# Second front of a hybrid attention and expert block: statistics, slot tables, row numbers and shared products in another order

## The reference, cut to what matters

```
x = x + attn_a(layernorm(x))      # a linear attention with decays, 16 heads of 8
x = x + ffn(layernorm(x))         # first feed-forward step
x = x + attn_b(layernorm(x))      # block attention on 5 levels, 16 heads of 64
x = x + ffn(layernorm(x))         # second feed-forward step, the same weights

def ffn(h):                                       # h: 2048 x 128
    shared = (silu(h @ shared_gate_w) * (h @ shared_up_w)) @ shared_down_w
    logits = h @ gate_w                           # 32 experts
    e, top = argmax(logits), max(logits)
    hs = h * sigmoid(top)
    routed = (silu(hs @ gate[e]) * (hs @ up[e])) @ down[e]
    return shared + routed
```

## Time and profile before

| what | value |
|---|---|
| runs | 557.72, 559.16, 559.17 us |
| profiled execution, its own time | 557.5 us |
| its span, first to last instruction | 555.6 us |
| TensorE busy | 495.6 us, 89% |
| VectorE busy | 425.7 us, 77% |
| ScalarE busy | 291.0 us, 52% |
| GpSimd busy | 251.4 us, 45% |
| mean granted TensorE clock | 0.979 |
| first products of the second loop | at 497.1 us |

### The profile page before, as it was taken

How to read it: one execution, slowest core, us unless ns; L and a number is a source line. 1 busy time by engine, 2 the same in 40 slices (tenths; PEclk the granted TensorE clock), 3 DMA queues, 4 the chain that set the end, 5 groups by cost and what they waited for, 6 DMA issues and landing times.

```text
span 555.6 us, 16703 instructions
## 1 busy us (share of the span) xinstructions
PE 495.6 (89%) x6472; PEld 304.0 (55%) x6472; DVE 425.7 (77%) x979; ACT 291.0 (52%) x624; POOL 251.4 (45%) x294
## 2 busy tenths in 40 slices
PE   6989888897989997999999999999999868989991
PEld 3323232355444443777767777777767655544540
DVE  3386968988747766868899888899878988847762
ACT  3544344254448864666545555446644433448870
POOL 3556777555514545253344443333233435633542
PEclk9999999999999999999999999999999988999996
DMA  6799920000269862100000000000000000169964
GB/s 183 313 425 283 99 21 0 2 0 20 76 190 268 271 216 72 30 4 21 21 21 22 22 22 22 22 21 21 22 21 8 7 2 11 42 187 275 276 217 139
DMA packets 45326, 54.11 MB, mean 97 GB/s; under 512 B 10880, under 2 KB 36416, under 8 KB 44224
## 3 DMA queue, kind: packets, MB, share of 16 engines
q1 hardware_dynamic: 42688, 47.78, 29.6%
q0 software_dynamic: 2560, 5.26, 2.7%
HBM read 43.55 MB, written 9.48 MB: 95 GB/s over the span
## 4 chain that ended last, share of the span: by engine, by line
PE 59%; DVE 24%; issue 6%; DMA 4%; POOL 3%; ACT 2%; DVEq 0%; SPq 0%; POOLq 0%; ACTq 0%
PE psum L1249 9%; PE psum L1730 7%; PE psum L1748 7%; PE psum L1823 5%; PE psum L1802 4%; PE psum L1268 4%; PE psum L1256 3%; DVE arena L761 3%; POOL sorted_x L1467 2%; PE psum L1771 2%; DVE arena L755 2%; PE psum L277 2%; PE psum L278 2%; DVE arena L2032 2%; DVE arena L2027 2%
## 5 line engine op out<-in xcount | busy, mean ns | idle before, releaser
L2202 POOL TENSOR_TENSOR arena<-arena 128x512 f32<-128x512 f32 x32 | 40.9, 1297 | 110.2 <-issue 103.0
L1495 POOL DMA_INDIRECT y_tok<-arena,to x48 | 46.6, 971 | 64.8 <-ACT arena L1318 63.4
L1918 ACT ACTIVATE arena<-psum 128x512 f32<-128x512 f32 x64 | 37.9, 597 | 45.2 <-PE psum L1730 42.0
L1730 PE MATMUL psum<-arena 128*128 128x512 f32 x128 | 59.2, 605 | 0.8 <-ACT arena L1901 0.7
L1249 PE MATMUL psum<-experts,arena 128*32 x96 | 50.2, 604 | 1.1 <-ACT arena L1308 1.1
L1249 PE MATMUL psum<-arena 128*32 128x512 f32 x288 | 50.9, 605 | 0.0
L661 POOL TENSOR_TENSOR arena<-arena 128x512 f32<-128x512 f32 x32 | 37.2, 1181 | 26.2 <-DVE arena L761 17.5
L1748 PE MATMUL psum<-arena 128*128 128x128 f32 x384 | 47.5, 278 | 1.4 <-ACT arena L1923 1.4
L1748 PEld LDWEIGHTS psum<-arena 128*128 128x128 f32 x384 | 45.2, 191 | 2.4 <-ACT arena L1923 2.4
L2139 POOL TENSOR_TENSOR arena<-arena 128x256 f32<-128x256 f32 (+4 forms) x75 | 33.9, 452 | 24.5 <-ACT arena L1937 17.9
L1730 PEld LDWEIGHTS psum<-arena 128*128 128x128 f32 x128 | 22.9, 189 | 35.6 <-issue 34.0
(11 more groups left out here) (240 smaller groups left out, 1204.1 us busy)
## 6 DMA issues: line engine op xcount, KB each, us to landing
arena<-in_experts SPq DMA_DIRECT2D x48, 384.0 KB, 4.4
experts<-in_experts SPq DMA_DIRECT2D x8, 1536.0 KB, 17.4
arena<-sorted_x SPq DMA_DIRECT2D x48, 64.5 KB, 3.8
sorted_x<-zeros SPq DMA_DIRECT2D x2, 1536.0 KB, 13.4
arena<-in_w_qkv SPq DMA_DIRECT2D x16, 192.0 KB, 3.4
arena<-y_tok SPq DMA_DIRECT2D x8, 256.0 KB, 3.1
x_tok<-in_x SPq DMA_DIRECT2D x4, 256.0 KB, 4.9
arena<-in_w_out SPq DMA_DIRECT2D x16, 64.0 KB, 1.9
```

The source lines that it names most:

```text
L1495: pool.indirect_dma_start(out=y_tok, out_offset=bass.IndirectOffsetOnAxis(ap=f_to[:, s:s + 1], axis=0), in_=f_gy[(s + 4) % 8], in_offset=N ...
L1730: pe.matmul(ring("in", n, j)[:, :], b_w[n % 2][:, which * P:which * P + P], x, start=True, stop=True)\
L1918: act.activation((b_q, b_k)[which][:, part * CHUNK:part * CHUNK + CHUNK], src, ACT.Copy, scale=(D_B ** -0.5, 1.0)[which]).then_inc(h["drai ...
L2202: pool.tensor_tensor(b_yn[:, part], b_y[:, part], b_rec[:, part], ALU.mult).then_inc(h["normed"], 1)
```

## The change

All of it is in the second front (k = 1) and in the last step of the second attention; the first front keeps its order. On TensorE one half of shared chunk 0 goes ahead of `project_out(15)`, the logits of chunk 2 go between the two turns, one half of shared chunk 1 goes ahead of the count, `shared_out(0)` goes behind the count, the two `keep_clock` products go, and the turn of line 1216 goes behind `shared_out(1)`. On GpSimd the second half of the last multiply of line 2202 goes; VectorE does it as `normalise_late`, with a signal of its own. On VectorE `first_slots` goes behind the statistics of chunk 3, one product of shared chunk 0 goes ahead of `gather_out`, `first_rows` goes behind the norm of chunk 3, and the search for the slots' experts, now a function `slot_experts`, goes behind `add_shared(0)` and the products of shared chunk 1. On ScalarE the second silu of shared chunk 0 goes ahead of the norm of chunk 2.

```
@@ TensorE, f_pe
                 front_turn(pe, k, 2)
+                front_logits(pe, k, 2)
                 front_turn(pe, k, 3)
-                front_logits(pe, k, 2)
                 front_logits(pe, k, 3)
+                shared_half(pe, k, 1, 0, 1)
+            count_tokens(pe, k, 1)
+            if k == 0:
+                shared_half(pe, k, 1, 0, 1)
+            else:
                 shared_out(pe, k, 0)
-            count_tokens(pe, k, 1)
-            shared_half(pe, k, 1, 0, 1)
             shared_half(pe, k, 1, 1, 2)
-            keep_clock(2)
+            if k == 0:
+                keep_clock(2)
             shared_half(pe, k, 2, 0)
+            if k == 1:
+                shared_out(pe, k, 1)
             done(pe, "slot_col", 1)
             pe.matmul(bank[7][0:1, 0:P], f_slot_col, ident, start=True, stop=True).then_inc(t["slot_row"], 1)
-            shared_out(pe, k, 1)
+            if k == 0:
+                shared_out(pe, k, 1)
@@ ScalarE, f_act
                 gate_shared(act, k, 0, 0)
+                gate_shared(act, k, 0, 1)
                 front_norm(act, k, 2)
-                gate_shared(act, k, 0, 1)
@@ VectorE, second_places: what followed row_numbers(dve, chain, a, 1) is now
+        def slot_experts(dve, chain, k):
+            before, a = half_of(k, 0), half_of(k, 1)
@@ VectorE, f_dve
                 row_ids(dve, k)
-                first_rows(dve, chain, k)
             c = STEPS - 1
...
             ins.then_inc(t["xn_last"], 1)
             if k == 1:
+                first_rows(dve, chain, k)
+                route(dve, chain, k, 2, 2)
+                product_shared(dve, k, 0, 1)
+                second_places(dve, chain, k)
+                add_shared(dve, k, 0)
                 for n in range(2):
-                    product_shared(dve, k, 0, n)
-                route(dve, chain, k, 2, 2)
+                    product_shared(dve, k, 1, n)
+                slot_experts(dve, chain, k)
@@ TensorE, project_out(n)
-                        pe.wait_ge(h["normed"], 2 * n + i // 4 + 1)
+                        if n == LAST and i:
+                            pe.wait_ge(h["normed_late"], 1)
+                        else:
+                            pe.wait_ge(h["normed"], 2 * n + i // 4 + 1)
@@ TensorE, last step of b_pe
+                    pe.wait_ge(h["y_out"], UNITS)
+                    shared_half(pe, 1, 0, 0)
                     project_out(n - 1)
-                    pe.wait_ge(h["y_out"], UNITS)
-                    for half in range(2):
-                        shared_half(pe, 1, 0, half)
+                    shared_half(pe, 1, 0, 1)
@@ VectorE, b_dve
+            def normalise_late():
+                part = slice(CHUNK, SEQ)
+                dve.wait_ge(h["y_out"], UNITS)
+                dve.wait_ge(h["o"], 2 * LAST)
+                dve.tensor_tensor(b_yn[:, part], b_y[:, part], b_rec[:, part], ALU.mult).then_inc(h["normed_late"], 1)
...
                 if n == UNITS:
-                    first_slots(dve, chain, 1)
+                    normalise_late()
+                    product_shared(dve, 1, 0, 0)
...
+            first_slots(dve, chain, 1)
             dve.wait_ge(h["acc"], 2 * LAST)
@@ GpSimd, b_pool_engine
-                for j in range(2):
+                for j in range(2 if n < LAST else 1):
```

More of the change, by code:

```diff
@@ L51 @@
 FOUND = 4
-SLOT_BOUND = "second_places keeps the expert of a slot between 0 and EXPERTS - 1"
+SLOT_BOUND = "slot_experts keeps the expert of a slot between 0 and EXPERTS - 1"
 ROW = C + 1
@@ L1374, in f_dve @@
                 route(dve, chain, k, 3, 1)
[L1375 to L1378, removed]
+                add_shared(dve, k, 0)
+                second_places(dve, chain, k)
+                slot_experts(dve, chain, k)
+                for n in range(2):
+                    product_shared(dve, k, 1, n)
             done(dve, "slot_row", 1)
@@ L1593, in hybrid_block @@
             "shift xn xt x pooled packed packed_odd ready coarse proj drained scored subbed turned expd weighed merged summed y_out z_out divided normed o biased "
-            "acc logits_in").split()}
+            "acc logits_in normed_late").split()}
         w_in, wo_in, bias_in = [sem(f"b_w_in{r}") for r in range(2)], [sem(f"b_wo_in{r}") for r in range(2)], sem("b_bias_in")
```

## The result

The changed kernel is slower. Its median is 561.79 us of 21 runs (559.59 to 564.21); the kernel before, run beside it, has 558.56 us of 21 (555.83 to 561.41). The ratio is 1.0058, with a 95% interval from 1.0043 to 1.0074: 3.2 us more. Of the versions further down, one run each of 3 (1660.38 us) and 11 (590.14) and one of the kernel before (967.94) were slow and are not in the ratios. The prediction had 559.2 us and no change as the likeliest case. The loss by late weight loads was in its sum, but at a size that cancelled against a gain.

A forecast was written before the change was run, and what follows sets the result against it. The landing of the last indirect write (493.82) lets the second loop start. GpSimd's gain of 0.6 us and SyncE's loss of 0.85 cancel, shift 0.0, so the median of 559.16 gives 559.2 us; range 556.8 to 561.0.

The forecast's parts named there:

- The attention's end: End of the second attention: `normalise_late` 1.31 us and a shared product 0.65 on VectorE; `gather_out` at 460.1, 1.25 earlier.
- `first_slots` in its new place: On VectorE behind chunk 3's statistics, without GpSimd's large multiply beside it: 1.9 us instead of 3.40, ending at 466.3.
- rival (c): Slower: `first_slots` keeps its 3.4 us and the last write lands 1.2 late, 560.4 us; chance 0.13.
- `placed` 1: VectorE's signal ahead of GpSimd's first eight writes: 1.7 us later, near 469.7, with the first write at 470.55.
- The turns and logits: Chunks 2 and 3 on TensorE in the second front: `route` starts at 470.9, gaining 1.05 us (0.45 to 1.6).
- the forecast's best case of 1.6: Turns and logits of the second front all at the full clock: `route` at 470.35, gain 1.6 us.
- GpSimd's queue as the bound: Sixteen writes without a pause: ninth at 481.3, 0.6 us earlier, last issued at 490.2; a pause before the ninth refutes it.
- Shared work last: Second front, search behind shared products: slots' row ready at 484.3, SyncE's weight loads start at 485.75, 0.85 us later.
- The landing: Last indirect write, issued 4.4 us after the loads' start, lands 8.1 after it, at 493.85 against 493.82 before.
- (a): Loads don't hold the writes: the last write lands 3.05 us after its issue, 558.6 to 558.0 us; chance 0.25.
- (b): Queue bounds fall altogether: ninth write follows `placed` 2 at its best, 1.6 earlier, with shorter fetch; 557.5 us; chance 0.15.
- Rival (d): Clock falls in TensorE's shared chain behind 1.35 us idle: 0.2 to 0.9 late, 559.4 to 560.1 us; chance 0.12.

The follow-up runs named there:

- 3: Changed kernel plus three products of 512 columns on TensorE in its idle time ahead of chunk 2's turn: ratio 1.0015 to the kernel before, median 559.17 us.
- 11: Version 5 (early search and products ahead of chunk 2's turn) timed again: ratio 0.9968 to the kernel before, median 557.57 us.
- 1: Changed kernel with the slots' experts searched early again and their row turned ahead of `shared_out(1)`: ratio 1.0003 to the kernel before, median 558.55 us.
- 2: Kernel before with only the late search of the slots' experts and their row turned behind `shared_out(1)`: ratio 1.0040, median 560.75 us.
- experiment 4: Changed kernel plus three products of 512 columns on TensorE between the last `shared_out` and the loop: ratio 1.0024 to the kernel before, median 560.02 us.
- 5: Changed kernel with the early search and three products on TensorE ahead of chunk 2's turn: ratio 0.9978 to the kernel before, median 558.14 us.
- 9: Changed kernel, search left late, with three products ahead of chunk 2's turn and three ahead of the loop: ratio 0.9995 to the kernel before, median 558.36 us.
- version 10: Changed kernel with early search, three products ahead of chunk 2's turn and the two `keep_clock` products put back: ratio 0.9985 to the kernel before, median 558.27 us.

## Why the prediction was wrong, point by point

- **The attention's end: right.** The half of chunk 0 took 1.88 in the gap, `normalise_late` 1.34 (1.31 forecast), and `gather_out` came at 459.54, which is 1.23 earlier when the offset of 0.58 at the entry is taken out (1.25 forecast).
- **`first_slots` in its new place: right.** From 463.86 to 465.74, 1.88 us (1.9 forecast). The scan took 0.68 and line 1092 0.19, so they are short away from GpSimd's multiply, and rival (c) falls. This agrees with the rule of the Trainium skill on the port pair of VectorE and GpSimd (SBUF — State Buffer, on the two separate sides of SBUF). So does `normalise_late`, which has two SBUF inputs, stands beside GpSimd's multiply and took 1.34, but no run shows it alone.
- **`placed` 1: right,** 469.1, and 469.7 with the offset, as forecast.
- **The turns and logits: the mechanism right, the term mis-sized.** The forecast had a stretch at the lower level from 467 to 470 and put `route` at 470.9. The clock fell as soon as forecast but stayed down until 477, through the logits of both chunks and the turn between. They took 1.70, 1.09 and 1.91. `route` started at 471.78, with the offset 472.4: no gain of 1.05 but a loss of 0.4. Experiment 3 shows that the clock was the whole of it: at the full clock `route` came 1.5 earlier than before, counted from the last `divide`, near the forecast's best case of 1.6.
- **GpSimd's queue as the bound: wrong,** since `placed` 2 came late. The pause of 1.33 us named as the sign of it is there. The last write was issued 0.5 later than forecast, 1.1 with the offset.
- **Shared work last: right.** The loads start 5.7 us behind the cast of `placed` 2 (5.8 forecast). In total they are 1.7 later than before, 2.3 with the offset, where 0.85 was forecast; the difference is the late `placed` 2.
- **The landing: this step failed.** I drew a line through two writes of one execution and read from it that a write issued 4.4 us after the loads' start lands 8.1 after that start. In the changed kernel the write issued 4.13 after it landed 9.49 after it. In versions 1 to 5, 9 and 11 the issue lies 4.1 to 5.7 after the loads' start and the landing 8.7 to 9.3, before it was 8.9. So it hardly depended on the issue and went with the loads' start. That it waits for the loads to drain is my reading of it and not shown: version 10, with 10.7, doesn't fit it, and in the changed kernel the DMA share (the last number but one of the rows below) falls from 0.73 to 0.15 and 0.03 while the write is still out; it lands at 496.10. What is gained in GpSimd's queue is worth nothing there. The delay of the loads, 1.69, is paid in full, and 0.6 on top, which no run explains. Of two writes in one queue the later one landed later for being later; the slope between them says nothing of moving the queue.

```profile
493.00:494.00 1.00, 0.77 (x6) 0.77 (x7) 1.00 (x3) 0.70 (x1) 0.00 (x0) 1.00 0.73 291
494.00:495.00 1.00, 1.00 (x11) 1.00 (x10) 0.59 (x2) 0.00 (x0) 0.00 (x0) 1.00 0.15 51
495.00:496.00 1.00, 0.29 (x3) 0.09 (x1) 0.68 (x1) 0.00 (x0) 0.00 (x0) 1.00 0.03 4
```

- **Rivals (a) and (b): not borne out.** The last write took 5.36 us from issue to landing, not the 3.05 of (a). For (b) `placed` 2 had to come 1.6 earlier, and it came no earlier than before.
- **The term that was missing, a second step that failed:** the idle time ahead of the loop and its clock, which the sum put at nothing. I had TensorE's chain end 1.0 us ahead of the fetch and took that for slack. It became 2.72 us idle, and the first two turns took 3.80 us of products instead of 2.07. From the loop's first product to the third turn's the changed kernel took 504.52 - 499.50 = 5.0, about 2.2 more than before. Rival (d) had the price of such a fall, but in the shared chain, where it didn't come.
- **Sum:** 2.3 of landing, 0.1 of a longer fetch and 2.2 of clock make the 4.6 us between the two profiled executions, where the forecast had 0.0. The medians differ by 3.2. The profiled execution of the kernel before, 557.5, was 1.1 below its median, so the pair shows more than the change costs; how the 3.2 divide is known only by experiment 4, some 1.9 for the clock ahead of the loop.

## What to carry to other kernels

Work put last on a path is not free when it releases transfers (here 1.7 us of later loads, 2.3 of later landing): ask which DMA the moved step starts, and what lands behind that DMA. A gap that becomes a wait of 2 to 3 us on TensorE costs twice, once as waiting and again as slower products behind it; a few idle products in it (here three of 512 columns) gave back some 1.9 us at one place and let an earlier result through at another. Filling one gap can leave the next one to do the same: in versions 3, 5, 9 and 11 the clock fell again a few us later. And a duration taken from neighbours in one queue is no law for moving the whole queue.

## What the runs showed of the hardware

- The last indirect write of the second front landed in 2.3 and 2.5 us with two weight loads of 384 KB ahead of it, and in 3.0 to 5.4 us with four. It landed 8.7 to 9.5 us after the start of the four loads in nine of ten executions, whether it was issued 4.1 or 5.9 us after it, and 10.7 in the tenth. In the first front of the same ten executions it was always issued 5.6 after the loads' start and landed 8.4 to 9.0 after it.
- Behind idle stretches of 3.14 and 2.72 us the granted clock fell from 1.0 to 0.50. It stayed there for about 10 and 7 us (466.8 to 477.1 and 497.5 to 504.4), much longer than the 3.4 us that followed the shorter gaps of the kernel before. Why isn't shown: of the 10 us, TensorE was busy without a break for the last 7.
- The length of one gap doesn't decide it. Behind an idle stretch of 1.49 us ahead of the count the clock fell in version 3 and stayed at 1.0 in version 10.
